# Decoder layer on one core: new order of attention, expert tiles of 256 and 128 rows, a last stage with a buffer for every chunk

## What is computed

```python
x = _layernorm(x + _L0_attn_ref(x, Wq, Wk, Wv, Wo, bo))      # 16 heads of 8, over groups of 64
x = _layernorm(x + _L0_xattn_ref(x, ctx_1024, ctx_1024))     # retention with decay mask
x = _layernorm(x + _L0_ffn_ref(x, gate, w1, w2, w3))         # 8 experts, top 2, inner size 512
```

## Time and profile before

| what | value |
|---|---|
| median of 3 runs | 934.62 us |
| the profiled execution, its own time | 931.58 us |
| its span, first to last instruction | 929.8 us |
| busy PE, DVE, ACT, POOL | 766.6, 763.4, 636.3, 542.8 us |
| mean granted TensorE clock | 0.928 of full speed |
| DMA traffic | 68.48 MB |

### The profile page before, as it was taken

How to read it: one execution, slowest core, us unless ns; L and a number is a source line. 1 busy time by engine, 2 the same in 40 slices (tenths; PEclk the granted TensorE clock), 3 DMA queues, 4 the chain that set the end, 5 groups by cost and what they waited for, 6 DMA issues and landing times. The chain is left out here.

```text
span 929.8 us, 34144 instructions
## 1 busy us (share of the span) xinstructions
PE 766.6 (82%) x11844; PEld 587.9 (63%) x11844; DVE 763.4 (82%) x2039; ACT 636.3 (68%) x1544; POOL 542.8 (58%) x439
## 2 busy tenths in 40 slices
PE   2577789999999999999877619999999999999400
PEld 2355556666666666666644308999999999999300
DVE  5898888999999999999886547887887887888466
ACT  1344367888889888889899707667667766766255
POOL 0365664588898888888864552444444444444354
PEclk9778799999999999999999859999999999999855
DMA  8511221222232222222230141222222222221276
GB/s 224 185 19 28 38 47 36 38 65 60 55 65 69 53 57 66 53 55 60 54 81 31 38 102 51 61 64 63 63 63 64 63 61 66 62 60 56 94 240 235
DMA packets 136740, 68.48 MB, mean 74 GB/s; under 512 B 74528, under 2 KB 125984, under 8 KB 136576
## 3 DMA queue, kind: packets, MB, share of 16 engines
q1 hardware_dynamic: 121440, 40.56, 18.8%
q0 software_dynamic: 8640, 17.84, 5.8%
q10 hardware_dynamic: 6496, 7.89, 2.8%
HBM read 37.91 MB, written 28.34 MB: 71 GB/s over the span
## 5 line engine op out<-in xcount | busy, mean ns | idle before, releaser
L1561 POOL TENSOR_TENSOR prod_ev<-e_sb,q_v 128x1024 f32<-128x1024 f32 x128 | 252.3, 2002 | 93.5 <-ACT e_sb L871 67.2
L1602 POOL DMA_INDIRECT token_halves<-w_new,tok_i x142 | 136.0, 958 | 189.7 <-DVE w_new L1504 167.8
L1577 POOL DMA_INDIRECT routed_rows<-xe,pos x128 | 130.4, 1018 | 72.8 <-DVE pos L1341 45.1
L1171 DVE TENSOR_TENSOR prod_qk<-q_v,QKV 128x2048 f32<-128x2048 f32 x64 | 145.9, 2280 | 3.3 <-PE SC L572 3.2
L1488 DVE TENSOR_TENSOR prod_ev<-prod_qk,prod_ev 128x1024 f16<-128x1024 f32 x71 | 87.0, 1226 | 56.2 <-ACT prod_ev L1051 56.2
L1051 ACT CAST prod_ev<-prod_qk 128x1024 f16<-128x1024 f32 x71 | 74.2, 1045 | 74.0 <-DVE prod_qk L1514 53.6
L780 PE MATMUL QKV<-k_t,w_hl 128*128 128x256 f16 x852 | 116.9, 274 | 0.0
L780 PE MATMUL ST<-k_t,w_hl 128*128 128x256 f16 x852 | 116.9, 274 | 0.0
L1060 ACT ACTIVATE prod_qk<-QKV,silu_scale 128x512 f32<-128x512 f32 x142 | 96.2, 678 | 10.2 <-PE QKV L780 6.7
L1514 DVE SCALAR_TENSOR_TENSOR prod_qk<-ST,hid_scale,prod_qk 128x512 f32<-128x512 f32 x142 | 99.4, 740 | 2.2 <-ACT prod_qk L1060 2.2
L932 ACT ACTIVATE q<-XT,tab 128x256 f32<-128x256 f32 x256 | 95.9, 473 | 4.2 <-PE XT L637 4.2
(11 more groups left out here) (168 smaller groups left out, 1557.9 us busy)
## 6 DMA issues: line engine op xcount, KB each, us to landing
w_new<-routed_rows SPq DMA_DIRECT2D x71, 130.0 KB, 2.2
prod_ev<-token_halves SPq DMA_DIRECT2D x16, 512.0 KB, 4.8
x_sb<-x SPq DMA_DIRECT2D x128, 32.0 KB
head_rows<-o_n SPq DMA_DIRECT2D x128, 32.0 KB
o_t<-head_rows SPq DMA_DIRECT2D x64, 64.0 KB, 2.7
ctx_sb<-ctx SPq DMA_DIRECT2D x32, 128.0 KB, 2.5
out<-prod_qk ACTq DMA_DIRECT2D x16, 256.0 KB, 4.0
token_halves<-w_new,tok_i POOLq DMA_INDIRECT x142, 2.2
```

The lines of the kernel that those rows point to most:

```text
L1171: eng.tensor_tensor(prod_qk[:, u, :, :].rearrange("p d (i j) -> p d i j", j=NH), q.unsqueeze(3).to_broadcast([P, HD, NH, NH]), k.unsqueeze ...
L1561: ins = eng.tensor_tensor(prod_ev[:, u, :, :, :, 0:HD].rearrange("p q j i d -> p (q j) i d")[:, n, :, :], e_sb[:, it.slot(2), u, :].rearra ...
L1577: eng.indirect_dma_start(out=xs, out_offset=bass.IndirectOffsetOnAxis(ap=pos[:, r, 2 * u + k:2 * u + k + 1], axis=0), in_=xe[:, r, u, k, : ...
L1602: eng.indirect_dma_start(out=halves, out_offset=bass.IndirectOffsetOnAxis(ap=tok_i[:, s, u:u + 1], axis=0), in_=yw[:, s, u, :], in_offset= ...
```

## The change

Six edits, made together.

1. **The order of stage A.** The lists of all engines are re-ordered and some lags change (PE's last is 20 instead of 19, ACT's 19 instead of 20). `wait_last` calls follow the new order. On SP load_heads comes right behind store_heads, and x is loaded one step before it was asked for.
2. **Start of stage A.** x of the first four duos is loaded before the small tables and before all three expert matrices, which SP now issues one after the other; DVE's bias work moves behind the first `products`, the blank `spare_rows` move to POOL, and ACT waits for them at the end of step 7 instead of step 1.
3. **Expert matrices.** Each raw matrix lies in a split buffer, so that a finished one gives its place to the next part; the splitting is done at steps 9 to 15; the maximum is spread through QKV instead of ST, and neither `queries_across` nor `ret_scores` waits for it. `blank_pad` goes from step 13 to step 42, into the buffer of `prod_qk`.
4. **Tiles.** 64 tiles of 256 rows and then 7 of 128. The table needs 51 dependent instructions.
5. **Stage C loads.** All 16 chunks have buffers of their own; the first four loads are single, the others are joined by two (1 MB).
6. **Stage C work.** POOL adds the halves; DVE takes the statistics, makes the shift and normalises one slice in four; ACT computes ln and exp for the -0.5 power (after loading its function table) and normalises three slices; SP stores, behind all its loads.

The weights are measured at steps 9, 10, 12, scaled at 10, 11, 13, and their low parts made at 11, 13, 15. The rest of the diff, cut to its core:

```diff
-    n_tiles = 2 * n_tok // TILE + n_exp - 1
+    n_whole, n_half = 2 * n_tok // TILE, n_exp - 1
+    n_tiles, n_more = n_whole + n_half, n_whole + n_half // 2
...
             load_x(Item(eng, None, None, 0))
             eng.dma_start(w_qkv_sb[:, :], w_qkv).then_inc(qkv_in, 16)
+            load_x(Item(eng, None, None, 1))
             eng.dma_start(tab[:, split:], table[:, split:]).then_inc(tab_in, 16)
+            for n in range(2, RING):
+                load_x(Item(eng, None, None, n))
             eng.dma_start(bo_sb[:, :], bo).then_inc(small_in, 16)
             eng.dma_start(wo_sb[:, :], wo).then_inc(small_in, 16)
             eng.dma_start(gate_sb[:, :], gate).then_inc(small_in, 16)
+            for n in range(3):
+                load_weights(n)
...
+        def part(n, low):
+
+            if low:
+                return (w1_hl, w3_hl, w2_hl)[n][:, 0, :]
+            return (w_new[:, 0:n_exp * inner // 2].bitcast(F16), w1_hl[:, 1, :], w3_hl[:, 1, :])[n]
...
+        def blocks_of(t):
+            return 2 if t.off < n_whole else 1
...
-                        mm = eng.matmul(out[:, 512 * half + TILE * n:512 * half + TILE * (n + 1)],
-                                        w_hl[:, wp, bass.ds(no * inner + P * (2 * half + n), P)], x_hl[:, x, xp, :],
+                        mm = eng.matmul(out[:, 512 * half + m * n:512 * half + m * (n + 1)],
+                                        part(w, wp)[:, bass.ds(no * inner + P * (2 * half + n), P)], x_hl[:, x, xp, 0:m],
...
+            def load_halves(at):
+                if (c := at(0)) and c.off < C_ALONE:
+                    eng.dma_start(halves_of(c), half_rows[:, C_SLICES * c.off:C_SLICES * (c.off + 1), :, :]).then_inc(load_of(c), 16)
+                elif c and c.off % 2 == 0:
+                    k = c.off % per
+                    eng.dma_start(fin[c.off // per][:, k:k + 2, :, :, :].rearrange("p c n k d -> p (c n) k d"),
+                                  half_rows[:, C_SLICES * c.off:C_SLICES * (c.off + 2), :, :]).then_inc(load_of(c), 16)
...
+            def store(at):
                 if c := at(0):
-
-                    wait(c, fout_ready, RING)
...
+                    wait(c, most_ready)
+                    wait(c, last_ready)
+                    eng.dma_start(out_rows[:, C_SLICES * c.off:C_SLICES * (c.off + 1), :], sum_of(c)).then_inc(fin_out, 16)
...
+                if c := at(0):
+                    wait(c, fmv_ready)
+                    eng.activation(fln[:, c.off, :], fmv[:, c.off, :, 1], ACT.Ln, bias=eps_c[:, 0:1]).then_inc(fln_ready, 1)
+                    wait(c, fln_ready)
+                    eng.activation(frs[:, c.off, :], fln[:, c.off, :], ACT.Exp, scale=-0.5).then_inc(frs_ready, 1)
+                if c := at(1):
                     wait(c, fnb_ready)
...
+                    for n in range(C_SLICES - 1):
+                        ins = eng.activation(sum_of(c)[:, n, :], sum_of(c)[:, n, :], ACT.Identity,
+                                             bias=fnb[:, c.off, n:n + 1], scale=frs[:, c.off, n:n + 1])
+                    ins.then_inc(most_ready, 1)
...
+            def add_halves(at):
+                if c := at(0):
+                    y = halves_of(c)
+                    eng.wait_ge(load_of(c), 16)
+                    eng.tensor_tensor(sum_of(c), y[:, :, 0, :], y[:, :, 1, :], ALU.add).then_inc(fsum_ready, 1)
```

606 lines of the change are left out of this document (327 added, 279 removed).

## The result

The changed kernel takes **921.81 us** (median of 3 runs, 920.71 to 923.54) against 934.62 before: ratio 0.986, interval 0.9821 to 0.9899. It is faster, but by a third of what was forecast (895.2 us), and it lies outside the range of 880 to 911.

The account below looks back on a forecast made before the run. Stage A at full depth was held bound by PE, DVE and POOL, each above 92% busy, and stage B by PE; stage C by none. Terms summed to -39.4 us, span 890.4, median 895.2 us, range 880 to 911.

Parts of the forecast that it names:

- Start, -9: Start of stage A: earlier x and delayed bias work bring the first two duos' products forward, saving 9 us.
- the bound of -2: Smallest gain allowed for the start of stage A, 2 us, if the later weight steps give it back.
- New order at full depth, -4: Stage A from 160 to 440 us: re-ordered lists recover about half the known waits, saving 4 us.
- The residual's 0.67 us a period should halve: Stage A at full depth: PE's wait for `o_t` before the residual product, 0.67 us a period, falls by half.
- Tail, 0 with bounds -3 and +2: End of stage A: a chain through masks, ACT and POOL's scatters, unchanged at 0 us, bounds -3 and +2.
- Slower: Rival, stage A at full depth: `max_of_four` behind `second_residual` waits each period, 2 us over 30 periods, total 959; chance 0.03.
- Table, +1.2: Between stages A and B: 51 linked table instructions instead of 22 become the gate to the first tile load, costing 1.2 us.
- Half tiles, -12.6: End of stage B: seven half tiles at 2.55 us each instead of 4.35, saving 12.6 us.
- The 59 ns: PE in stage B: time of one product of 128 columns, used to price a half tile's 36 products.
- Last tile, -4.5: End of stage B: a half-size last tile shortens its serial chain and drops one scatter, saving 4.5 us.
- Stage C, -10.5: Stage C: traffic and engine chain both limit at about 41.5 us; taken as 41.4 for 51.9, saving 10.5 us.
- Stage C is two phases: Rival, stage C: SP's stores queue behind all loads, so the stage takes 46 us, total 900; chance 0.12.

Follow-up runs that it names:

- k8: Kernel after the change with all engines' step lists of stage A put back to those before, everything else kept; 918.12 us.
- k18: Kernel after with PE's, DVE's and ACT's stage A lists as before the change, SP's kept new (heads loaded right behind their stores); 900.96 us, ratio 0.9631.
- k1: Kernel after with `second_residual` moved behind `max_of_four`, `divide` and `subtract_max` in DVE's stage A list; 923.01 us, ratio 0.9874.
- k21: Kernel before the change with one edit in SP's stage A list, `load_heads` right behind `store_heads`; 917.04 us, ratio 0.9808.
- k5: Kernel before the change with `second_residual` put ahead of `max_of_four` and `divide` in DVE's list; ratio 1.0105.
- k7: Kernel after with PE's sums ahead of `ret_scores`, `second_residual` behind `divide` and `subtract_max`, and the padding blank behind stage A's last step; 921.79 us.
- k23: k18 with the blank of the padding rows moved from DVE's step 42 to POOL's step 42; 897.97 us, ratio 0.9618.
- k4: Kernel after with PE taking expert 0's matrices at fixed addresses in the last tiles, leaving out the choice of the right expert; 911.2 us.
- k3: Kernel after with the seven half tiles loaded and computed as whole tiles, their second half not scattered; stage B 324.0 us, profiled span 925.5 us.

## Why the prediction was wrong, step by step

*Start, -9:* measured -4.3. Failed step: "Without both they start at 6.3 + 4.0 = 10.3 us." It took PE's list as it was; in the new one the transposes of duo 1 stand ahead of the projection and wait 2.3 us for their x. k8 and k18, with the old list, start at 10.34 and 10.38. That is not the whole miss. The products of duo 1 were forecast near 18.5 and come at 21.61; in k8 they come at 19.87, after 1.5 us of waiting for the scores of duo 0, which the sum did not have. By duo 9 k8 and k18 are ahead of the kernel after by no more than 0.6 and 1.5 us (128.37 and 127.47). From duo 1 to duo 9 the kernel after takes 107.4 us and the kernel before 106.4, where the sum had some 0.6 less instead of 1.0 more: the steps with the weights gave part of the start back, as the bound of -2 allowed. No run prices them apart.

*New order at full depth, -4:* the size holds (-1 and -5 in two profiles against the kernel before, -5 to -10 against k8), the reason does not. "The residual's 0.67 us a period should halve" failed: the wait stayed at 10.5 us (8.7 in the repeat). SP gave the 0.6 to 1 us of the sum (from the first store of the heads to their load the median is 5.1 us before and 4.2 after), but the later `divide` used it up. k1 shows that: with `divide` first the wait is 0.9 us. Had I priced the edits apart, SP's list would have been worth both waits of the earlier trace rows, 15 us and not 4 to 5: k21 gives 12.4. When PE no longer waits for `o_t`, DVE's wait for PE (5.5 us) goes too: the same delay handed on, as the prediction had read it.

*Tail, 0 with bounds -3 and +2:* measured +12.5, the largest miss. Failed step: "Six lists end as they did." No row of the tail stood under it, while the order had just moved `second_residual` ahead of `divide`. At full depth a loop of 12.9 us hides in a period of 13.3 to 13.8; in the tail, where the masks of the kernel before come 8.7 to 10.8 us apart, it is the limit. In the kernel after three of these steps take 12.7, 15.3 and 11.0 us instead of 10.8, 9.9 and 9.5, some 9 us of the 12.5 (the 1.8 us of the blank lie in the second). The other 3 to 4 come later, where no residual runs any more; no run prices them. This is my rival "Slower" at another place: its mechanism (an entry of DVE's list behind `second_residual`) was right, for `divide` rather than `max_of_four`, and I let it count at full depth only. That a closed loop of such kind makes the tail long is shown by k5 (+9.7 by one edit), that the new lists of PE, DVE and ACT together make it long by k18. Why k1 and k7 did not shorten it is read from their traces, not tested: `norm_shift` and the gates close the same loop once `second_residual` is late. The blank in step 42 is worth 3 us by k23, against 0 to 1.8 in the prediction, but tails of one program differ by as much.

*Table, +1.2:* measured +1.0, and the table is the gate. Right.

*Half tiles, -12.6:* measured -1.3. Failed step: "Two engines at 2.3 and three waits between them make 2.55." The 59 ns were right (57 in k4), and so was 2.55 as the pace of data (2.52 to 2.8 us in the steps of k4 and k19 shown above). What was not in the sum is PE's own instruction stream: it works out the experts' addresses in registers, with 27 register instructions a step for a half tile and for a whole one alike. In whole tiles they must lie under the products of 256 columns, as the 59 ns of the 24 down-products suggest, on which the term rests; no run shows that part by itself. The Trainium skill (TensorE: Matmul & The Clock Gate, Back-to-back issue gap) gives about 81 ns for products of 128 columns in a real stream. The kernel after shows 82, but k4 shows 57 with the same products, so here it is not the products' limit.

*Last tile, -4.5:* some 4, within its bounds. k3 gives 5 to 6 us for both terms together, and the 1.3 of the seven steps are taken off.

*Stage C, -10.5:* measured -10.3, but the number is luck. Failed step: "with the wait between them and the hops 2.0 us a chunk". ACT needs 1.6 (its logarithm 0.30, its exponential 0.21, three slices 1.25, overlapping a little), and DVE, which I had with room to spare, takes 2.5 a chunk as long as POOL's additions last, for half of the chunks. The two errors cancel. The rival "Stage C is two phases" was near in its order of traffic, not in its price: at 905 us 9.6 of 12.6 MB had moved, all the loads among them, but the first stores were issued at 889.9 us and the end came after 41.6 us, not 46. The Trainium skill (SBUF — State Buffer, SBUF: two separate sides) says that DVE and GpSimd share one pair of ports under an exclusive lock, which a DVE operation needs in a two-port mode or with two SBUF inputs. The trace agrees: the scaling takes 0.31 us against 1.12, the shift (L1635, two inputs) 0.14 against 0.46, and the statistics, with one input, the same in both. In which mode the scaling ran the trace does not show.

## What to carry to other kernels

Price each moved entry alone, against the queue it feeds: a load placed right behind its store was worth 12 to 16 us with the old lists around it, and was hidden by other entries moved with it. When a list's order is changed, follow each new "stands behind" until it closes on itself, and hold that loop against the shortest period of the kernel (the tail), not against the full-depth one. A loop can have several links of one length, and then taking out one of them changes nothing. Halving the tiles saved 1.3 us of 12.6, since PE's stream was filled with address arithmetic; count register instructions beside the products.

## What was not expected of the hardware

A register instruction in PE's stream cost at least 0.1 us where the stream was the limit (16 of them against 1.6 us a step), more than a product of 128 columns with its weight load (0.057 us). The same DVE instruction took 3.6 times as long beside POOL's additions. Two profiles of one program differed by 4 us in a stretch of 300, lost in single steps.
